# Four graph layers on one core: a deferred last sum, a second block of rows masked where it lands, and a reordered opening of pass 4

## The reference: what is computed

```python
x = _layernorm(x + _L0_gnn_ref(x, adj, adj, W1, f1, W2, f2))   # adj @ (f * (adj @ (x @ W))), twice, relu between
x = _layernorm(x + _L1_gnn_ref(x, adj, beta))                  # attention, below
x = _layernorm(x + _L2_gnn_ref(x, adj, ...))                   # GRU cell on relu((adj @ x) @ W_msg.T + b_msg)
x = _layernorm(x + _L3_gnn_ref(x, adj, W_self, W_neigh))       # x @ W_self + (adj @ x / deg) @ W_neigh

# _L1_gnn_ref
cos = beta * (x @ x.T) / (norm2 @ norm2.T + 1e-07)
masked = cos + (1.0 - adj) * -1000000000.0
P = jax.nn.softmax(masked, axis=1)
return P @ x
```

## Time and profile before

| | |
|---|---|
| median of 3 runs | 1717.4 us (1713.45 to 1720.19) |
| the profiled execution: its own time, its span | 1712.72 us, 1710.9 us |
| PE busy | 1650.5 us (96%) |
| DVE busy | 1377.6 us (81%) |
| ACT busy | 1236.7 us (72%) |
| POOL busy | 235.4 us (14%) |
| DMA | 461.61 MB, mean 270 GB/s |
| granted clock of PE, mean | 0.992 of full speed |

### The profile page before, as it was taken

One profiled execution on the slowest core, in us unless ns is written; L12 is line 12 of the kernel. 1 busy time (PEld: TensorE's weight loads), 2 busy tenths in 40 slices (PEclk: granted clock), 3 DMA queues, 4 the chain that ended last, 5 costly groups with the idle time before them and its releaser, 6 DMA issues.

```text
span 1710.9 us, 22249 instructions
## 1 busy us (share of the span) xinstructions
PE 1650.5 (96%) x8530; PEld 1376.0 (80%) x8530; DVE 1377.6 (81%) x1518; ACT 1236.7 (72%) x1251; POOL 235.4 (14%) x258
## 2 busy tenths in 40 slices
PE   7999999999999999978999999999899999999996
PEld 6888888888888887757999999999778767767885
DVE  6888887788878977776877878788788887787897
ACT  6776766676767766867787778787767777676775
POOL 0000000000000000166333333333330000000000
PEclk9999999999999999998999999999999999999998
DMA  9999999899989997963433344433569957848995
GB/s 393 381 375 370 377 340 373 292 370 368 360 297 383 370 364 275 331 232 144 149 139 122 134 148 148 149 143 127 210 198 357 348 178 249 292 163 287 354 332 170
DMA packets 63136, 461.61 MB, mean 270 GB/s; under 512 B 6672, under 2 KB 10928, under 8 KB 11312
## 3 DMA queue, kind: packets, MB, share of 16 engines
q1 hardware_dynamic: 63024, 460.14, 72.7%
HBM read 458.00 MB, written 2.11 MB: 269 GB/s over the span
## 4 chain that ended last, share of the span: by engine, by line
PE 84%; DVE 8%; ACT 4%; DMA 2%; issue 2%; POOL 0%; DVEq 0%; SPq 0%; ACTq 0%; POOLq 0%
PE ps L1183 18%; PE ps L1174 18%; PE ps L1177 18%; PE ps L1266 6%; DVE aL L794 4%; PE ps L1281 3%; PE ps L1283 3%; PE ps L1282 3%; PE ps L1251 3%; PE ps L1253 3%; PE ps L1252 3%; ACT aH L483 2%; DMA raw<-adjT 2%; DVE ptL L976 1%; PE ps L1213 1%
## 5 line engine op out<-in xcount | busy, mean ns | idle before, releaser
L794 DVE TENSOR_TENSOR aL<-raw,aH 128x2048 fp32r<-128x2048 f32 (+1 forms) x364 | 826.9, 2275 | 178.1 <-ACT aH L483 175.3
L483 ACT ACTIVATE aH<-raw 128x2048 fp32r<-128x2048 f32 (+1 forms) x364 | 689.9, 1899 | 260.5 <-PE ps L1177 173.0
L1174 PE MATMUL ps<-aH,yH 128*128 128x512 f32 x1472 | 408.4, 399 | 12.5 <-ACT aH L483 12.3
L1183 PE MATMUL ps<-aL,yH 128*128 128x512 f32 x1472 | 399.2, 393 | 12.2 <-DVE aL L794 12.2
L1177 PE MATMUL ps<-aH,yL 128*128 128x512 f32 x1472 | 395.4, 390 | 0.0
L1183 PEld LDWEIGHTS ps<-aL,yH 128*128 128x128 f32 x1472 | 273.7, 188 | 81.7 <-DVE aL L794 26.3
L1174 PEld LDWEIGHTS ps<-aH,yH 128*128 128x128 f32 x1472 | 271.5, 188 | 76.9 <-issue 19.4
L1177 PEld LDWEIGHTS ps<-aH,yL 128*128 128x128 f32 x1472 | 276.6, 188 | 58.8
L976 DVE TENSOR_TENSOR ptL<-ps,ptH 128x512 fp32r<-128x512 f32 x256 | 176.6, 690 | 87.9 <-ACT ptH L617 85.4
L617 ACT ACTIVATE ptH<-ps 128x512 fp32r<-128x512 f32 x192 | 114.3, 595 | 83.8 <-PE ps L1266 78.0
L414 POOL TENSOR_SCALAR raw<-raw 128x2048 f32<-128x2048 f32 x64 | 122.3, 1912 | 260.9 <-ACT raw L531 260.5
(11 more groups left out here) (146 smaller groups left out, 1675.8 us busy)
## 6 DMA issues: line engine op xcount, KB each, us to landing
raw<-adjT SPq DMA_DIRECT2D x364, 1024.0 KB, 5.9
raw<-adj SPq DMA_DIRECT2D x30, 2048.0 KB, 8.3
raw<-adj SPq DMA_DIRECT2D x4, 1024.0 KB, 6.8
kept<-adjT SPq DMA_DIRECT2D x4, 1024.0 KB, 12.0
xT<-norms SPq DMA_DIRECT2D x1, 2048.0 KB, 6.9
out<-xrow SPq DMA_DIRECT2D x8, 256.0 KB, 4.8
xrow<-x_rows SPq DMA_DIRECT2D x1, 1024.0 KB, 14.7
xrow<-x_rows SPq DMA_DIRECT2D x1, 768.0 KB, 9.1
```

The costliest lines, as they stand in the source:

```text
L483: ins = nc.scalar.activation(a_tiles(q, t)[0][:, cols], a_source(q, t)[:, cols], ACT.Copy)
L794: ins = dve.tensor_tensor(low[:, cols], a_source(q, t)[:, cols], high.bitcast(F32)[:, cols], ALU.subtract)
L1174: pe.matmul(b, block(yH, k), high[:, c], start=(k == 0), stop=False)
L1183: ins = pe.matmul(b, block(yH, k), low[:, c], start=False, stop=(k == NB - 1))
```

## The change

Four parts:

1. **The deferred sum.** The sum of a super block's last batch is issued in batch 0 of the next super block, behind its transposes and scores; the very last one stands behind the last super block. On ACT, `o_copy` moves behind the `turned_high` and the last `exponent` of batch 0.
2. **Super block 1 masked where it lands.** Its two row blocks are loaded into `kept[:, 2]` and `kept[:, 3]`, where its masked scores go too (`mask_row`), as soon as pass 3 has used the tiles there. SP issues these loads before it waits for the norms; the norms leave from `xT` instead of `kept`. ACT sums row block 2 before the first exponents, and POOL makes its bias right behind `stage_unit(1, 0)`.
3. **Pass 4's opening.** ACT splits tile 4 before the last `o_copy`. The layer norm's steps on DVE move from tiles 5 and 6 to 8 and 11, `root` from 6 to 10, the two `normalise` from 8 and 10 to 13 and 15, and what hangs on them (ACT at 11 and 12, DVE's `low` at 12 and 13) to 16 and 17, and 17 and 18.
4. **Pass 3.** Steps 3 to 7 of the first half's layer norm move from tile 11 of the second half to tile 12 on DVE, and the four `UNIT_AT` steps one tile on.

```diff
@@ tables
-    UNIT_AT, X1_AT = (13, 15, 18, 20), (25, 27)
-    X2_LOW_AT = {4: 5, 5: 7, 6: 12, 7: 13}
+    UNIT_AT, X1_AT = (14, 16, 19, 21), (25, 27)
+    X2_LOW_AT = {4: 5, 5: 7, 6: 17, 7: 18}
-        uT = kept[0:NB, 2, 0:D]
+        uT = xT[0:NB, 0:D]
+        def mask_row(sbi, r):
+            return rows_of[2 + r] if sbi == 1 else rowbuf[:, r, :]
@@ SP
+            for r in range(2):
+                sp.wait_ge(tile_used, gn(3, SPLIT_ONCE[2 + r]) + 1)
+                sp.dma_start(mask_row(1, r), adj_rows[2 + r]).then_inc(row_landed[r], 16)
             sp.wait_ge(uT_ready, 1)
             sp.dma_start(norms, uT).then_inc(u_written, 16)
...
-            for sbi in range(1, NSB):
+            for sbi in range(2, NSB):
@@ POOL
             stage_unit(1, 0)
+            for h in range(2):
+                mask_bias(1, 0, h, 5 + h)
             normalise(1, HBK + 1)
             low_of_x(4, X1_BY_ACT + 1)
             stage_unit(1, 1)
-            for h in range(2):
-                mask_bias(0, h, 5 + h)
             normalise(1, HBK + 2)
             normalise(1, HBK + 3)
             for c in range(HBK, BK):
                 low_of_x(4, c)
                 if c == HBK + 1:
                     for h in range(2):
-                        mask_bias(1, h, 7 + h)
+                        mask_bias(1, 1, h, 7 + h)
@@ ACT
             high_of_x(1, X1_BY_ACT + 1)
+            for h in range(2):
+                degrees(2, h)
...
                 for k in range(NBATCH):
-                    if k == 0 and before:
-                        o_copy(sbi - 1)
                     if k not in HIGH_BY_DVE:
                         turned_high(sbi, k)
                     if k + NBATCH - first_r1 < NCH and before:
                         exponent(sbi * 2 + 1, 2 * parity + 1, k + NBATCH - first_r1)
+                    if k == 0 and before:
+                        o_copy(sbi - 1)
...
                     exponent(r, r, c)
-                    if r == 1 and c >= 2:
-                        degrees(2, c - 2)
...
             super_block(NSB - 1, 1, 0, True)
+            split_high(4, EARLY_TILES)
             o_copy(NSB - 1)
...
             for t in range(EARLY_TILES, TILES):
-                split_high(4, t)
-                if t == 6:
+                if t > EARLY_TILES:
+                    split_high(4, t)
+                if t == 10:
                     root(3, EARLY_LN, NB)
-                if t in (8, 10):
+                if t in (13, 15):
@@ DVE
-                        if u == 11:
+                        if u == 12:
                             for i in range(3, SCALE_STEPS):
                                 scale_step(i, 0, HBK, 0, NB // 2)
...
-                dve.tensor_tensor_reduce(row[:, c * CH:(c + 1) * CH], S2[m % 2], rowbuf[:, r, c * CH:(c + 1) * CH],
+                dve.tensor_tensor_reduce(row[:, c * CH:(c + 1) * CH], S2[m % 2], mask_row(sbi, r)[:, c * CH:(c + 1) * CH],
...
                 if t == 5:
                     o_stats(NSB - 1)
+                if t == 8:
                     for i in range(3):
                         scale_step(i, 3, BK + NB, EARLY_LN, NB)
-                if t == 6:
+                if t == 11:
                     for i in range(3, SCALE_STEPS):
@@ PE
                     if k >= 1:
                         sum_batch(sbi, k - 1, before)
+                    elif before:
+                        sum_batch(sbi - 1, NBATCH - 1, sbi >= 2)
                     if k == 2 and before:
                         turn_sums(sbi - 1, second)
-                sum_batch(sbi, NBATCH - 1, before)
...
             super_block(NSB - 1, 0, True)
+            sum_batch(NSB - 1, NBATCH - 1, True)
```

More of the change, by code:

```diff
@@ L350, in _ @@
             sp.wait_ge(urow_landed, 16)
-            for sbi in range(1, NSB):
+            for sbi in range(2, NSB):
                 for r in range(2):
                     sp.wait_ge(m_ready, masks_of_row(sbi - 1, r))
-                    sp.dma_start(rowbuf[:, r, :], adj_rows[sbi * 2 + r]).then_inc(row_landed[r], 16)
+                    sp.dma_start(mask_row(sbi, r), adj_rows[sbi * 2 + r]).then_inc(row_landed[r], 16)
             for r in range(2):
@@ L409, in stage_unit, with mask_bias @@
                 pool.tensor_tensor(wL[:, r, :], tmp, wH[:, r, :].bitcast(F32), ALU.subtract).then_inc(bw_ready, 1)
-            def mask_bias(r, h, nth):
+            def mask_bias(sbi, r, h, nth):
                 pool.wait_ge(deg_done, nth)
-                t = rowbuf[:, r, h * HALF:(h + 1) * HALF]
+                t = mask_row(sbi, r)[:, h * HALF:(h + 1) * HALF]
                 pool.tensor_scalar(t, t, -1.0, MASK, ALU.add, ALU.mult).then_inc(bias_ready, 1)
@@ L421, in _ @@
             normalise(1, X1_BY_ACT)
-            mask_bias(0, 0, 1)
-            mask_bias(1, 0, 2)
+            mask_bias(0, 0, 0, 1)
+            mask_bias(0, 1, 0, 2)
             normalise(1, X1_BY_ACT + 1)
@@ L431, in _ @@
             ins.then_inc(unit_by_pool, 1)
-            mask_bias(0, 1, 3)
-            mask_bias(1, 1, 4)
+            mask_bias(0, 0, 1, 3)
+            mask_bias(0, 1, 1, 4)
             pool.wait_ge(unit_by_dve, 2)
@@ L457, in _ @@
                     for h in range(2):
-                        mask_bias(r, h, (sbi * 2 + r) * 2 + h + 1)
+                        mask_bias(sbi, r, h, (sbi * 2 + r) * 2 + h + 1)
             pool.wait_ge(rstd_ready, 3)
@@ L732, in _ @@
             for t in range(EARLY_TILES, TILES):
-                split_high(4, t)
-                if t == 6:
+                if t > EARLY_TILES:
+                    split_high(4, t)
+                if t == 10:
                     root(3, EARLY_LN, NB)
-                if t in (8, 10):
+                if t in (13, 15):
                     act.wait_ge(rstd_ready, 4)
-                    normalise(X2_BY_POOL + (t - 8) // 2, x_by_act)
-                if t in (11, 12):
-                    high_after_sums(X2_BY_POOL + t - 11)
+                    normalise(X2_BY_POOL + (t - 13) // 2, x_by_act)
+                if t in (16, 17):
+                    high_after_sums(X2_BY_POOL + t - 16)
                 if 8 <= t < 8 + 2 * BK and t % 2 == 0:
@@ L947, in mask_chunk @@
                     dve.wait_ge(urow_landed, 16)
-                    corr = row[:, c * CH:(c + 1) * CH]
+                    corr = rows_of[2 * (sbi % 2) + r][:, c * CH:(c + 1) * CH] if sbi != 1 else rowbuf[:, r, c * CH:(c + 1) * CH]
                     dve.tensor_scalar(corr, xT[:, c * CH:(c + 1) * CH], epsu[:, rb:rb + 1], 1.0, ALU.mult, ALU.add)
```

## The result

The changed kernel takes 1705.44 us (median of 5 runs, 1703.07 to 1706.95) against 1717.4 for the kernel before (5 runs): a ratio of 0.9928, with a 95% interval of 0.9909 to 0.9947. The forecast was 1705.3. Of the profiled executions, 1712.72 became 1705.44 us and the span 1710.9 became 1703.6.

The account below looks back on a forecast made before the run. PE was taken to set the pace in the steady attention and to wait in pass 4's opening. Gains 5.9 + 4.2 + 2.0 + 0 = 12.1 us off the median 1717.4 gave 1705.3 us, range 1702 to 1708.5.

Parts of the forecast that it names:

- The seam: At each super block's end PE loses 0.39 us to a stop and an unhidden weight load; 15 boundaries give 5.9.
- the cover of `o_copy`: At a super block boundary, `o_copy` on ACT ends 0.3 us before the sum of batch 0 needs the accumulator.
- the last two: The last two super block boundaries, where PE waits for ACT and DVE anyway, may give 0.3 us more or less each.
- the rival: `o_copy` takes the stop's place at all 15 boundaries alike; part 1 gone if 0.3 plus 0.39 us late; chance 0.04.
- the first stop: In the attention's opening, PE waits about 2.3 us for the first `ptL` after the change.
- the second stop: In the attention's opening, PE waits about 3.6 us for row block 3, until about 788.5 us.
- A slow stretch behind the second stop: Attention's opening: PE's clock falls in the second wait, costing 2.7 us; total gain 9.4, time 1708.0; chance 0.17.
- lower bound of 2.6: Part 2's gain, attention's opening, if POOL's 1.61 us wait for `yH` stays; as a rival 1706.9 us, chance 0.06.
- The stops that were to go: Pass 4, tiles 4 to 6: 0.85 us and 0.80 of 1.07 go, 1.45 stays; 2.0 us taken with exposed steps.
- the moved steps, costed as hidden: Pass 4's layer norm steps, moved to later tiles, cost nothing; gain 0.9 us if they stop PE once.
- the four signs that the prediction had named against itself: PE waiting for `o_copy`; clock 0.50 after 786 us; DVE not waiting for row block 3's bias; ACT late, tiles 10 to 18.
- The step from the profiled execution to the median: Whole kernel: the profiled execution, 1712.7 us, lies 4.7 below the median 1717.4, so 1700.6 becomes 1705.3.

Follow-up runs that it names:

- Part 1 alone: The kernel before with only the deferred sum and the moved `o_copy`: 1709.66 us, ratio 0.9946.
- the run with `o_copy` first: The changed kernel with `o_copy` put back ahead of batch 0's `turned_high` and exponent, sums still deferred: 1719.18 us, ratio 1.0006.
- half the wait: The changed kernel with the first half of row block 3's bias ahead of two `low_of_x` on POOL: 1701.45 us; second execution 1704.87 us.
- the last run: The kernel of together with the first half of row block 3's bias one `normalise` earlier on POOL: 1699.85 us, ratio 0.9886.
- The run with the bias first: The changed kernel with row block 3's bias ahead of two `normalise` and two `low_of_x` on POOL, ACT's last two `high_of_x` later: 1708.15 us, ratio 0.9948.
- part 2 alone: The kernel before with only super block 1 masked where it lands: 1714.55 us, ratio 0.9978.
- three edits: The run with the bias first, plus last `o_rows` and `o_stats` one tile later and the last super block's `o_copy` before the exponent: 1707.86 us, ratio 0.9946.
- the second of the changed kernel: The changed kernel itself measured once more, nothing altered: 1704.60 us, ratio 0.9924.
- together: Run before the last run: half the wait, last `o_rows` and `o_stats` one tile later, last super block's `o_copy` before the exponent: 1700.27 us, ratio 0.9896.

## Why the prediction was right

**Part 1, 5.9 us forecast, 6.8 measured.** The seam is worth 0.40 us at each of 13 boundaries, as worked out, and the cover of `o_copy` is 0.35 where 0.3 was forecast. What was off is the size of the last two, "0.3 more or less each": from sum 12 to the next super block's sum 12 the last two distances fell from 30.94 and 30.82 to 30.13 and 30.02, 0.8 each, so that the whole lies above the upper bound of 6.6. Part 1 alone gives the same. Nor are the 15 boundaries alike for `o_copy`, as the rival had it: at the last one the cover is gone and PE waits 0.77 us for it, which costs less than the 1.07 that it waited for `ptL` before. That the deferral pays only with the moved `o_copy` is shown by the run with `o_copy` first; `o_copy` moved without the deferral was not run.

**Part 2, 4.2 forecast, 2.3 and 3.8 measured.** The mechanism held: the first stop is 2.12 us (2.3 forecast), the second 3.60 (3.6), and the bias of row block 3 starts 0.4 us later than worked out. That POOL's order sets the second stop is shown by the runs that change this order alone: half the wait against the changed kernel (where the clock fell behind the first stop in both, the second stop is 1.75 us in the changed kernel and gone with half the wait), and the last run against the one before it (1.20 us and gone; the moved `o_rows` and `o_copy` stand in both). The run with the bias first also moved ACT's `high_of_x`; this put 3.86 us of idle time into POOL's queue, and PE stopped for the next thing that POOL owes. The step that failed is the weight of the clock. A slow stretch behind the second stop had a chance of 0.17 and a price of 2.7 us; in three of four executions of kernels with this order of POOL (the changed kernel once, part 2 alone, `o_copy` first) it came, and the gain fell to 2.3, below the lower bound of 2.6. Its price was 1.5 us (51.50 against 49.97): the stretch lasted some 3.4 us, where the price had been taken from the 5.46 us of PE's work in 772 to 782. In the fourth it came behind the first stop and cost nothing, as the prediction had said of that case. The Trainium skill (TensorE: Matmul & The Clock Gate, Part 1: The HAM clock gate) says that the clock is set by how busy the engine has been of late, with throttled as the default; by that the longer stop should be the one with a slow stretch behind it. The traces agree for the five stops of 3.38 to 3.83 us between 780 and 830 us, behind each of which the clock stood at 0.50, but a slow stretch followed the shorter first stop too, in 4 of 10 executions.

**Part 3, 2.0 forecast, 2.2 and 2.5 measured.** The stops that were to go went, 1.45 stayed (1.46) and the last is 0.17 (0.27 forecast). Two errors met: the stops with their exposed steps gave 2.6, and the moved steps, costed as hidden, let 0.1 to 0.5 be lost again at tile 16, where ACT came late.

**Part 4, 0 forecast, 0.0 to 0.1 measured**, and 1.0000 by time when alone.

**The sum.** 12.1 forecast; 11.2 and 13.0 in the four middle pieces of the two executions; 12.0 by the medians, with an interval of 9.1 to 15.6. The first part came out 0.9 higher, the second 0.4 to 1.9 lower and the third 0.2 to 0.5 higher, so that the total came within 0.1 us is in part luck: errors of opposite sign, inside a wide interval. Three of the four signs that the prediction had named against itself came, each at a small price: PE waiting for `o_copy` (at the last boundary alone), a granted clock of 0.50 after 786 us (at about 790 on the clock of before), and ACT late at tile 16. The step from the profiled execution to the median (4.7 us) was right, and the likely reason is one that the prediction didn't give: that execution was the earliest of 14 in its first 650 us, 5.4 us below their median.

## What to carry to other kernels

Where one engine's queue bounds a stage, removing a wait can move it to the next thing which that queue owes; write down the due time of each before reordering, and count the idle time that the reorder itself puts into the queue. The deferred sum paid only with the copy that frees its accumulator deferred too. And compare pieces of the trace between one and the same instruction: here some tenths of a microsecond could be told in a piece, while the time of a run moved by 10 us.

## What the runs showed of the hardware

The landing of the tiles differs between executions of unchanged code. ACT's waits from 20 to 640 us, in the execution before and in that of part 1 alone (us in total, times, longest):

```profile
ACT aH L483 <- DMA raw<-adjT: 48.0, 58, 3.0
```

```profile
ACT aH L483 <- DMA raw<-adjT: 89.5, 89, 2.8
```

The second reaches the first mark 11.4 us later. What makes the tiles land later was not tried.

The clock is not a fixed answer to a stop: behind the same first stop of 2.1 us PE was slowed for about 3.4 us in 4 of 10 executions (both of half the wait, three edits, and the second of the changed kernel). Stops of 1.75 us (the changed kernel's second execution) and 1.20 us (together) later in the same stage were not followed by a slow stretch. What decides at 2.1 us stays open.
